# Two small attentions of a decoder: each projection by TensorE issued in two halves, in two neighbouring steps

## The reference, cut to what matters

```
x = LN(x + attn0(x))                      # own code, not touched
q = rope(x @ Wq); k = rope(ctx @ Wk); v = ctx @ Wv      # c0
x = LN(x + softmax(q k^T / 4) v @ Wout + bout)
x = LN(x + ffn0(x))                       # not touched
q = x @ Wq; k = x @ Wk; v = x @ Wv        # a1, causal
x = LN(x + softmax(q k^T / sqrt(32)) v @ Wo + bo)
x = LN(x + xattn1(x, ctx)); x = LN(x + ffn1(x))         # not touched
```

## Time and profile before

| | |
|---|---|
| profiled execution, its own time | 3220.54 us |
| its span, first to last instruction | 3218.7 us |
| PE busy in the span | 2812.4 us, 87% |
| DVE, ACT, POOL busy | 64%, 55%, 46% |
| exponentials of c0, first to last start | 774.80 to 1213.87 us |
| exponentials of a1, first to last start | 1884.07 to 2158.48 us |

### The profile page before, as it was taken

How to read it: one execution, slowest core, us unless ns; L and a number is a source line. 1 busy time by engine, 2 the same in 40 slices (tenths; PEclk the granted TensorE clock), 3 DMA queues, 4 the chain that set the end, 5 groups by cost and what they waited for, 6 DMA issues and landing times. The chain is left out here.

```text
span 3218.7 us, 64393 instructions
## 1 busy us (share of the span) xinstructions
PE 2812.4 (87%) x24738; PEld 1994.4 (62%) x24738; DVE 2067.4 (64%) x4863; ACT 1768.8 (55%) x3780; POOL 1464.8 (46%) x1555
## 2 busy tenths in 40 slices
PE   5999999967888887999999978888999999975787
PEld 3666666644666665777777756666666766753343
DVE  6677777767777765655555547766555565555886
ACT  4555555546888884333333257765444444454896
POOL 3444444435888884544444425551111122212686
PEclk8999999988999987999999989999999999997899
DMA  5000000001000013000000011002001110012000
GB/s 172 27 1 2 1 1 1 1 9 35 2 2 2 2 48 94 27 8 8 1 1 1 1 50 41 21 2 76 14 28 39 40 40 1 1 62 80 23 21 27
DMA packets 47125, 81.75 MB, mean 25 GB/s; under 512 B 5731, under 2 KB 15973, under 8 KB 46693
## 3 DMA queue, kind: packets, MB, share of 16 engines
q1 hardware_dynamic: 46820, 77.64, 7.4%
HBM read 73.44 MB, written 4.19 MB: 24 GB/s over the span
## 5 line engine op out<-in xcount | busy, mean ns | idle before, releaser
L1146 POOL TENSOR_TENSOR c_pT<-c_prob,c_pT 128x512 f16<-128x512 f32 x256 | 293.7, 1160 | 64.6 <-ACT c_pT L1096 63.3
L2029 POOL TENSOR_TENSOR c_prob<-c_prob,c_inv 128x512 f32<-128x512 f32 x128 | 133.4, 1044 | 302.6 <-DVE c_inv L2247 302.6
L789 DVE SCALAR_TENSOR_TENSOR a_pT<-psT,a_kvh_t,a_pT 128x256 f16<-128x256 f32 (+1 forms) x256 | 94.6, 411 | 169.2 <-ACT a_pT L695 169.2
L1339 ACT ACTIVATE c_prob<-psT 128x512 f32<-128x512 f32 x256 | 156.4, 611 | 72.5 <-PE psT L1268 52.8
L1146 POOL TENSOR_TENSOR a_pT<-a_prob,a_pT 128x384 f16<-128x384 f32 x128 | 120.8, 950 | 157.8 <-ACT a_pT L1096 157.4
L1423 DVE TENSOR_REDUCE c_peak<-psS 128x2 f32<-128x512 f32 x256 | 167.1, 683 | 13.5 <-PE psS L1249 11.4
L1096 ACT CAST c_pT<-c_prob 128x512 f16<-128x512 f32 x256 | 160.1, 626 | 0.0
L488 POOL TENSOR_TENSOR a_q_rot<-a_q_cos,a_q_sin 128x512 f32<-128x512 f32 x64 | 86.8, 1357 | 159.6 <-DVE a_q_sin L808 159.6
L2163 ACT ACTIVATE c_prob<-c_prob,c_negmax 128x256 f32<-128x256 f32 x256 | 128.1, 502 | 56.0 <-DVE c_negmax L2239 55.0
L507 POOL TENSOR_TENSOR a_prob<-a_prob,a_inv 128x128 f32<-128x128 f32 x128 | 52.6, 411 | 221.6 <-DVE a_inv L782 221.6
L1679 POOL TENSOR_TENSOR f_ch<-f_h,f_c 128x256 f32<-128x256 f32 x88 | 76.4, 868 | 142.3 <-DVE f_h L1896 142.3
(11 more groups left out here) (626 smaller groups left out, 11341.0 us busy)
## 6 DMA issues: line engine op xcount, KB each, us to landing
c_feed<-in_L_ffn_w1T SPq DMA_DIRECT2D x16, 512.0 KB, 3.7
c_feed<-in_L_ffn_w2T SPq DMA_DIRECT2D x16, 512.0 KB, 3.7
x_all<-in_x SPq DMA_DIRECT2D x8, 512.0 KB, 7.0
a_ring<-in_L_attn_WqT SPq DMA_DIRECT2D x8, 512.0 KB, 5.7
a_ring<-in_L_attn_WoutT SPq DMA_DIRECT2D x8, 512.0 KB, 4.0
a_feed<-in_L_xattn_Wq SPq DMA_DIRECT2D x8, 512.0 KB, 3.8
c_feed<-in_L_xattn_Wo SPq DMA_DIRECT2D x8, 512.0 KB, 4.4
c_feed<-in_L_ffn_w3T SPq DMA_DIRECT2D x8, 512.0 KB, 3.6
```

The lines of the kernel that those rows point to most:

```text
L789: last = dve.scalar_tensor_tensor(pT[1][:, r, m, m * P:N], T[:, m * N + m * P:(m + 1) * N], kvh_t[:, b % 2, m, H + h:H + h + 1], pT[0][:, ...
L1146: pool.tensor_tensor(pT[1][:, c % NPH, :], prob[:, c % NPX, :], pT[0][:, c % NPH, :], ALU.subtract)\
L1339: act.activation(prob[:, c % NPX, :], ST[c % 2][:, 0:EW], ACT.Exp).then_inc(s.e_done, 1)
L2029: pool.tensor_tensor(prob[:, h % NPB, :, :], prob[:, h % NPB, :, :], inv[:, h % NPB, :].rearrange("p (n a) -> p n a", a=1).broadcast_to([P ...
```

## The change

A projection's matmuls over the weights' row blocks are cut in two. The first half of a piece of step `t+1` is issued at the end of step `t`, with its wait for the bank in front of it; the second half is issued in step `t+1`, at its old place among the pieces, and signals `bank_ready`. Transposes stay whole. The loop begins one step earlier, on all engines.

```diff
+    HALVED = ("q", "k", "v", "kv", "y")
-        FIRST, LAST = -H + min(0, at["k0"] if from_ctx else at["x0"]), (B + 1) * H + 5
+        FIRST, LAST = -H + min(0, at["k0"] if from_ctx else at["x0"]) - 1, (B + 1) * H + 5
...
-                def project(b, kind, n):
+                def project(b, kind, n, half):
...
-                    for k in range(K):
+                    for k in range(half * K // 2, (half + 1) * K // 2):
                         last = three(pe, out, a[0][:, k, rows], a[1][:, k, rows], w[0][:, k, cols], w[1][:, k, cols],
                                      k == 0, k == K - 1)
-                    last.then_inc(s.bank_ready, 1)
+                    if half == 1:
+                        last.then_inc(s.bank_ready, 1)
-                def output(b, n):
+                def output(b, n, half):
                     pe.wait_ge(*is_free("o", b, n))
-                    for k in range(KE):
+                    for k in range(half * KE // 2, (half + 1) * KE // 2):
...
-                    last.then_inc(s.bank_ready, 1)
+                    if half == 1:
+                        last.then_inc(s.bank_ready, 1)
...
                     for kind, b, n in pieces_at(t):
+                        if kind in HALVED:
+                            if kind == "y":
+                                output(b, n, 1)
+                            else:
+                                project(b, kind, n, 1)
+                            continue
                         if use[kind, b, n] >= 2:
                             pe.wait_ge(*freed[use[kind, b, n] - 2])
...
+                    for kind, b, n in pieces_at(t + 1):
+                        if kind in HALVED:
+                            if use[kind, b, n] >= 2:
+                                pe.wait_ge(*freed[use[kind, b, n] - 2])
+                            needs_weights(pe, kind, b)
+                            if kind == "y":
+                                output(b, n, 0)
+                            else:
+                                project(b, kind, n, 0)
```

More of the change, by code:

```diff
@@ L1301, in _ @@
                     for kind, b, n in pieces_at(t):
+                        if kind in HALVED:
[4 more added lines that the diff above has]
+                            continue
                         if use[kind, b, n] >= 2:
                             pe.wait_ge(*freed[use[kind, b, n] - 2])
-                        needs_weights(pe, kind, b)
                         if kind == "sk" and b == 0 and n == 0:
```

## The result

The kernel after takes 3241.35 us (median of 5 runs, 3235.97 to 3244.04), the one before, measured beside it, 3221.95 (5 runs, 3216.84 to 3222.93): a ratio of 1.0063, 95% interval 1.005 to 1.0077. The forecast of slower was right; 3231 was too small by 10 us, and 3241 lies outside the range. The profiled execution of after took 3244.04 us with a span of 3242.2, some 2.7 above its median, so the two traces differ by 23.5 us where the medians differ by 19.4.

What follows compares the result with a forecast made beforehand. No engine is full throughout c0's batch: PE, then DVE, then POOL bounds it; in a1 PE is nearly full. 10.3 + 1.1 - 1.0 - 0.6 - 2.8 + 1.8 = +8.8 us gave 3231, range 3222 to 3239.

Steps and rivals of the forecast that it cites:

- The waits in front of the first halves: Loaded c0 batch: PE waits about 1.4 us before v0, 0.4 before v1, 1.8 before k1, delaying scores.
- The plain price of them: Full c0 batch, read at POOL: held-up steps cost +2.05 us, 10.3 over batches 1 to 5.
- The bounds, +0.50 and +2.75: Full c0 batch: +0.50 us if POOL absorbs k1's stall, +2.75 if the exponential's whole shift counts.
- The halves level the load: y0, y1 in c0: banks free in time, but PE has no gap to fill, so no gain counted.
- In the sum I keep one such stretch, as before.: c0: one batch keeps its stretch at 1.2 GHz, as batch 3 had (1.64 us longer); no clock term added.
- Rival 3: c0 at k1: PE's 1.84 us wait lowers the clock in all five batches, +6.6 us, 3237; chance 0.12.
- q0, kv1, q1, y0 and y1 find their banks free within 0.1 us: a1: only kv0 waits (0.6 us, partly recovered), so +0.3 for each of 6 batches, +1.8.
- Small terms: Outside c0's batches 1 to 5: lead-in -2.8, batch 0 -0.6, batch 6 +1.1, batch 7 -1.0 us.
- The lead-in: Start of c0: first halves of k0, q0, q1 fill PE's waits for DVE, -2.8 us.
- Rival 1: c0: levelling wins, halves cut POOL's waits behind y0, y1, k0; -10.5 us plus lead-in, 3209; chance 0.08.
- rival 2: c0: POOL or ACT make up the waits, 2.5 us in place of 10.3, so 3223; chance 0.22.
- Rival 4: Whole kernel: halves stand back to back without other work between, time as before, 3222; chance 0.02.

Runs made afterwards that it cites:

- the filler: The changed kernel plus 10 unneeded matmuls of 240 columns ahead of v0's first-half wait in c0, batches 2 and on: 3232.88 us, ratio 1.0033.

## Why the prediction was right in its direction and wrong in its size

The traces differ by 23.5 us, the sum by 8.8. c0 with its lead-in took 13.2 us more where 7.0 was forecast, a1 9.7 where 1.8 was; so two steps failed, one in each.

- **The waits in front of the first halves: right.** v0 waits 1.26 us, k1 1.13, and the next exponential is held up by both. v1 was to wait 0.4 us; with the filler it waits 0.27, in after not at all, as PE gets there later.
- **The plain price of them: too high by 0.6 us a batch.** +2.05 was forecast, +1.43 measured at full clock. v0 (0.88 forecast, 0.78), v1 (0.42, 0.39) and k0 (-0.60, -0.61) were right. The miss is k1, from 0.50 to 2.05 at POOL, so 1.55: measured 0.91. The working had k1's first half waiting 1.8 us; it waited 1.13. x0 was read out when the working said (43.9 us into the batch with the filler, 43.6 forecast), but PE got there 1.0 us later than that. The bounds, +0.50 and +2.75, held.
- **"The halves level the load", for y: no gain.** It was left at nothing in the sum, and that was right (56.89 without, 56.88 with): the halves of y only move POOL's waits, which from steps 13 to 20 make 5.2 us in sum with them and without.
- **The first step that failed, in c0: "In the sum I keep one such stretch, as before."** The added term for the clock was zero, and it measured 10.6 us in c0, 8.4 of them in batches 1 to 5, more than all waits there (5 x 1.43 = 7.2). Rival 3 had the mechanism and a fair price (1.64 a batch; with the filler as the yardstick it is 1.0 to 2.2), but put it at k1, which is not needed for it: it lies at v0's wait. Its 3237 was nearer than the forecast.
- **The second, in a1: "q0, kv1, q1, y0 and y1 find their banks free within 0.1 us".** +1.8 forecast, +9.7 measured. That sentence holds in batch 3 and was carried over to the others. y1's half waits 1.01 us in batch 5 for DVE, behind a conversion, and makes 4.9 us in all, 2.5 of them with a stretch at 1.2 GHz; q0's waits 0.43 and costs 0.9. kv1 and y0 cost 2.5 although their banks are free: that an early half costs nothing where its bank is free was wrong too. kv0, the one wait that was foreseen, came as sized: 0.61 us, and +1.6 in the batches behind batch 0.
- **Small terms.** The lead-in was right (-2.6 for -2.8). Batch 0 won 2.4 rather than 0.6, by luck: with no half in c0 it took as little (51.02) when the clock stayed up, so the halves gave it nothing that the runs can tell. Batch 6 costs +2.0 with the filler (53.42), not 1.1, and 2.2 more without; 0.8 of it is q's (52.24 with q0 and q1 alone, 51.45 before), a term that the sum lacks. Batch 7 gave nothing: it took 43.0 or 44.6 us with y's halves and without them.
- **Luck.** That k1 was priced too high and batch 0's gain was the clock's covered some 5 us of what the two steps left out.

Rival 1 fell for the whole change (k1 and v0 do wait), yet k0's half alone does what it says, and rival 2's making up holds only for kv0, in batches 1, 2 and 5. Rival 4 has nothing for it.

## What to carry to other kernels

Splitting a group of matmuls pays only for a half whose bank is free when TensorE gets there: a half that waits stands in front of independent work in an in-order queue and turns a hidden wait into an open one. A free bank is no promise either: kv1's and y0's halves in a1 find theirs free and cost 2.5 us. So choose piece by piece; here 3 of 14 places won 0.2%, and all 14 lost 0.6%. Where a kernel's rows already show a batch at lower clock behind a wait, price a new wait ahead of dense work at its length and at that batch's extra time, with a real chance for each; and read a bank's release in every batch that has other work on the releasing engine, not in one.

## What the runs showed of the hardware that was not expected

Between the granted clock and a wait there is no fixed price. The same 1.26 us in front of v0 was followed by a stretch at 1.2 GHz in each of batches 1 to 6 of after, in every second batch when c0's first scores began 6 us earlier (749.95) with the same code of c0, in four of batches 1 to 5 with v0, q0, q1 and k0, and in one of them without k1's half or with v0 alone. Ten matmuls of 240 columns in that wait, 1.19 us, kept the clock up behind it in all six batches with all halves. What decides between a wait that is followed by the lower clock and one that is not stays open: rows with the same waits, one after the other, show both.

Nor is such a stretch always a loss. With v whole the clock was 0.50 from 885.8 to 892.4 us, at the start of batch 2, and the batch took 57.78 us like the others; with k0 alone in halves, where no first half waits in a loaded batch, it was 0.50 from 833.0 to 839.7, and that batch took 59.68 where its neighbour took 56.95. So a batch time is compared only between batches whose stretches are known.

The Trainium skill, "TensorE: Matmul & The Clock Gate", section "A second HAM failure mode: psum-queue depth-cycling", says that small gaps between groups of matmuls that cycle through PSUM banks can make the clock swing. The trace of after agrees (0.91 to 0.94 in each loaded batch); the kernel with v0 alone, whose batches 3 to 5 stay at 1.00 with the same gap, does not.
